# One product in place of two where a half block's edges are spread over the position one-hots

## The reference

```python
xn = _layernorm(x)
h = xn @ W_layer.T + b_layer
a1, a2 = h @ w_a1.T + b_a1, h @ w_a2.T + b_a2
v = leaky_relu(a1[src] + a2[dst], negative_slope=0.01)
ev = exp(v - segment_max(v, src)[src])
gnn = segment_sum((ev / segment_sum(ev, src)[src])[:, None] * h[dst], src)
x = x + gnn + linear_attention(xn)        # 8 heads, features elu + 1
x = x + slice_attention(_layernorm(x))    # 8 heads, 64 slices
```

## Time and profile before

| | us |
|---|---|
| median of 3 runs | 1741.72 (1740.88 to 1742.45) |
| the profiled execution | 1743.75 |
| its span, first to last instruction | 1741.9 |
| PE busy | 1405.2 |
| DVE busy | 1340.7 |
| POOL busy | 1133.4 |
| ACT busy | 662.8 |

### The profile page before, as it was taken

One profiled execution on the slowest core, in us unless ns is written; L12 is line 12 of the kernel. 1 busy time (PEld: TensorE's weight loads), 2 busy tenths in 40 slices (PEclk: granted clock), 3 DMA queues, 4 the chain that ended last, 5 costly groups with the idle time before them and its releaser, 6 DMA issues. The chain is left out here.

```text
span 1741.9 us, 27653 instructions
## 1 busy us (share of the span) xinstructions
PE 1405.2 (81%) x8473; PEld 1112.0 (64%) x8473; DVE 1340.7 (77%) x4033; ACT 662.8 (38%) x1867; POOL 1133.4 (65%) x1196
## 2 busy tenths in 40 slices
PE   5449888885598888898888888888888888887699
PEld 3237777764477666676666666666666666765487
DVE  8898999994488777788777777778777877884244
ACT  0014434340355444454444444444444444441000
POOL 0038888886777777777777777777777777740000
PEclk8659999996599999999999999999999998998599
DMA  9801111112344444444444444444444444520722
GB/s 93 147 5 57 51 46 57 45 52 55 105 121 120 119 121 120 120 119 120 120 123 117 120 121 116 117 121 118 115 120 121 120 117 119 146 69 23 293 74 74
DMA packets 118355, 180.11 MB, mean 103 GB/s; under 512 B 41727, under 2 KB 90238, under 8 KB 118207
## 3 DMA queue, kind: packets, MB, share of 16 engines
q0 software_dynamic: 44384, 113.26, 25.0%
q1 hardware_dynamic: 62735, 45.22, 12.3%
q10 hardware_dynamic: 11088, 19.87, 3.1%
HBM read 142.98 MB, written 35.29 MB: 102 GB/s over the span
## 5 line engine op out<-in xcount | busy, mean ns | idle before, releaser
L1043 POOL DMA_INDIRECT big<-node_table,rest x850 | 857.6, 1009 | 245.6 <-issue 231.5
L1114 PE MATMUL psum<-big 128*125 128x257 f32 x1700 | 428.2, 409 | 79.4 <-DVE big L1613 79.4
L1114 PEld LDWEIGHTS psum<-big 128*125 128x125 f32 x1700 | 337.8, 204 | 142.0 <-DVE big L1613 86.3
L1262 ACT ACTIVATE rest<-big,rest 128x125 f32<-128x125 bf16 x850 | 267.5, 489 | 146.3 <-DVE rest L1561 146.3
L337 POOL DMA_INDIRECT edge_groups<-rest x112 | 141.8, 1266 | 79.6 <-DVE rest L760 52.1
L1613 DVE TENSOR_SCALAR big<-big,rest 128x125 f32<-128x125 bf16 x850 | 171.7, 290 | 0.0
L1568 DVE TENSOR_REDUCE rest<-rest 128x125 f32<-128x2125 f32 x50 | 118.3, 2367 | 32.5 <-ACT rest L1262 32.5
L1142 PE MATMUL psum<-rest,big 125*128 125x126 f32 x416 | 74.1, 333 | 72.0 <-DVE big L1532 72.0
L1142 PEld LDWEIGHTS psum<-rest,big 125*128 125x128 f32 x416 | 63.5, 233 | 90.8 <-DVE big L1532 89.6
L1253 ACT COPY big<-psum 125x1024 bf16<-125x1024 bf16 x150 | 103.7, 762 | 38.1 <-PE psum L1091 38.1
L1149 PE MATMUL psum<-big 125*128 125x256 f32 x416 | 101.0, 386 | 0.0
(11 more groups left out here) (390 smaller groups left out, 2714.4 us busy)
## 6 DMA issues: line engine op xcount, KB each, us to landing
big<-node_table,rest POOLq DMA_INDIRECT x850
slice_weights<-rest ACTq DMA_DIRECT2D x52, 252.0 KB
big<-slice_weights ACTq DMA_DIRECT2D x25, 252.0 KB, 6.9
big<-slice_weights SPq DMA_DIRECT2D x25, 252.0 KB, 7.2
node_table<-big SPq DMA_DIRECT2D x50, 126.0 KB
normalised_turned<-big SPq DMA_DIRECT2D x50, 125.0 KB
rest<-normalised_turned SPq DMA_DIRECT2D x50, 125.0 KB, 2.4
out_dram<-rest SPq DMA_DIRECT2D x50, 125.0 KB
```

Source lines behind the costliest of these rows:

```text
L1043: pool.indirect_dma_start(Gt[:, u, q * TW:(q + 1) * TW], None, table, bass.IndirectOffsetOnAxis(ap=item[:, u, 2 * q:2 * q + 1], axis=0)).t ...
L1114: mm = pe.matmul(bank[bAgg][0:R, 0:D + 1], P[:, u, q, :], Gt[:, u, q * TW:q * TW + D + 1], start=q == 0, stop=q == Q - 1)
L1262: act.activation(V[:, :, q], O[:, u, q, 0:R], ACT.Copy, scale=score[:, u, q:q + 1]).then_inc(s_v, 1)
```

## The change

`spread` makes both halves of `moved` by one instruction of 28 x 128 = 3584 elements per partition instead of two of 28 x 64 = 1792. Its first input is `pos_hot`, read twice for each column (once per digit); its second is the pair of digits, each repeated over 64 positions. For this the digits of an edge stand side by side in one tile `codes` (low, low, high, high), of which `low2` and `high2` are now views; L649, L651 and the memsets of the unused columns write through them. `moved_made` counts two per half instead of three.

```diff
-            low2, high2 = b.take(128, JW, 2, dtype=F16), b.take(128, JW, 2, dtype=F16)
+            codes = b.take(128, JW, 4, dtype=F16)
+            low2, high2 = codes[:, :, 0:2], codes[:, :, 2:4]
...
                     def put(n, h):
-                        pe.wait_ge(moved_made, 3 * (2 * n + h + 1))
+                        pe.wait_ge(moved_made, 2 * (2 * n + h + 1))
...
                         if n + 1 < NB:
-                            pe.wait_ge(moved_made, 3 * (2 * n + 1))
+                            pe.wait_ge(moved_made, 2 * (2 * n + 1))
                             block_starts(n + 1)
...
                     def spread(k, h):
-                        dve.wait_ge(moved_made, 3 * (2 * k + h))
+                        dve.wait_ge(moved_made, 2 * (2 * k + h))
...
                         dve.wait_ge(hot_pos, 2 * k + h + 1)
-                        for f, of in enumerate((low2, high2)):
-                            dve.tensor_tensor(twos(moved[:, h, :, 64 * f:64 * (f + 1)]), twos(pos_hot),
-                                              pairs(of[:, at, :], HW, 64), ALU.mult).then_inc(moved_made, 1)
+                        dve.tensor_tensor(moved[:, h].rearrange("p j (f a b) -> p j f a b", f=2, b=2),
+                                          twos(pos_hot).unsqueeze(2).to_broadcast([128, HW, 2, 32, 2]),
+                                          codes[:, at].rearrange("p j (f b) -> p j f b", f=2).unsqueeze(3).to_broadcast(
+                                              [128, HW, 2, 32, 2]), ALU.mult).then_inc(moved_made, 1)
```

## The result

| | before | after |
|---|---|---|
| median, 18 runs each, same chip (us) | 1741.54 (1738.41 to 1745.35) | 1745.89 (1742.45 to 1751.77) |
| profiled execution, span (us) | 1741.9 | 1745.5 |
| mean granted clock of TensorE | 0.910 | 0.911 |
| last scatter of the sort ends (us from the start) | 417.1 | 420.6 |
| start of one block to the next, mean from 157 to 390 us | 23.21 | 23.75 |

The changed kernel is slower: its time is 1.0024 of the one before, 95% interval 1.0015 to 1.0034, or 4.3 us. Forecast were 1732.0, and a range of 1728 to 1742; the result lies above it. The sign was wrong. The difference arises in the sort: its last scatter ends 3.5 us later, the first gather of the item loop starts at 427.2 for 424.2, and the span ends 3.6 later.

A forecast was written before the change was run, and what follows sets the result against it. VectorE was taken to set the sort's period. Its saving of 11.0 us (product and stalls), less 1.3 given back in POOL's last block, left 9.7 us: 1732.0 us from the median of 1741.72, range 1728 to 1742.

The forecast's parts named there:

- The product itself: Spread on DVE: one product of 3584 elements takes 2.02 us, saving 0.14 us a block.
- the operand forms: Merged product's new repeated operands: keep L741's pace, 2.02 us; far bound 4.07 us at one element per step.
- the layout: L649 and L651 writing pairs in steps of four: nothing to 1.78 us each, before an idle 6.53 us, costing nothing.
- Rival 2: Merged product on DVE falls to one element per step, 4.07 us: 53 us on top, 1785 us; chance 0.05.
- The stalls: DVE's spread beside POOL's products: four stalls of 0.53 us a block become two; 1.15 us saved in eight blocks.
- The 11 us on the spread of VectorE: VectorE's saving up to the last block: 8 x 1.15 + 3 x 0.55 + 0.14 = 11.0 us.
- POOL is then 1.1 us late: POOL at the next block's first L349: 18.75 us, where it could go at 17.65; the lateness doesn't grow.
- the 21.7 that I forecast: Sign in a middle block of the sort: a period near 21.7 us.
- Rival 3: POOL becomes the bound, let in later at two vanished boundaries: 0.63 us more a block, 1749 us; chance 0.08.
- its deciding point: POOL's lateness passing 1.9 us, within which L349 is still inside the first L741; the replay stays at 1.06.
- PE must follow: PE's second put: 0.98 us of idle room, late by at most 0.16 us, so 1.06 to 1.22 us saved a block.
- The tail: Last block of the sort: POOL's scatters end it and come late, giving back 1.3 us; range 0 to 2.5.

The follow-up runs named there:

- order of three: Changed kernel with POOL's scatters issued three instead of two behind each unit: 1730.33 us, 0.9928 of the kernel before; a second run 1728.63 us, 0.9911.
- third buffer: Changed kernel with three instead of two buffers for the scatters' edges and slots: 2351.39 us on the slower chip, 1.0015 of the kernel before, sort 411.1.
- quiet merged kernel: Changed kernel with POOL's two tensor products per unit cut to one column of 256: 2327.94 us, 0.9922 of the kernel before, sort 398.4.
- filled kernel: Changed kernel with 24 small products on PE ahead of its wait for the first half: 2366.86 us, 1.0048 of the kernel before, sort 420.8.

## Why the prediction was wrong, point by point

- *The product itself, the operand forms, the layout*: right. 2.02 us undisturbed, 2.55 with a stall; the layout alone changed nothing. Rival 2 is out.
- *The stalls*: right for the spread. Four a block became two, 24.2 us became 12.4, the last product is never stalled, POOL's waits fall as replayed. The 11 us on the spread of VectorE were there (11.8 by the stalls).
- *The step that failed* is the sentence that POOL is then 1.1 us late and that this "doesn't grow, because POOL's operations from that boundary on, none of them shut out, end 11.8 us later". I replayed only DVE's long instructions and asked whether POOL's lateness comes back to them. POOL came where the replay had it: the unit's products were to start 18.75 us after the block's start and start at 18.79 (197.62). But DVE is at another place by then: it is 1.2 us earlier (L756 at 17.99, before L754 at 19.18). This opens two costs that the sum didn't have. The first is the short instructions of the unpack and of split_places, stretched by 0.5 to 0.8 us each, 2.34 in a long block, 8.9 in the sort for 2.7 before. The unpack had POOL's products beside it before, too, and what differs is a fraction of a microsecond: in the block of the earlier trace rows L756 (223.83) started 0.16 us before the end of L349 (223.27 to 223.99), and L757, the next, 0.10 ahead of L353 (224.07); now L759 starts 0.07 us behind the start of a product and is held until its end. The second is the wait of L771 for the last scatter's landing, 8.4 us in the sort for 1.7 before. The rows for that wait, 221.74, 224.22 and the landing after 2.1 us, were in the trace of before, 0.38 us of room; the prediction didn't use them and nowhere named `scattered`, by which DVE waits for POOL.
- *How much the two are.* From the changed kernel to its order of three (the first run) the sort is 16.6 us shorter: 7.7 are the wait of L771 (8.4 to 0.7), 7.1 the stalls on short instructions (8.9 to 1.8), and the rest, under 2, is the ranks and the end of the sort. The wait was also taken away alone, by the third buffer; the stretched short instructions never were, and their part is by this account of the rows. The steady period there, 21.53, lies just below the 21.7 that I forecast; that is another kernel than the one forecast, and bears out the replay of the spread, not the forecast.
- *Rival 3* had the sign and was near in size (1749, with a chance of 0.08), the size by luck. Its mechanism was POOL late by the vanished boundaries, which is right, and its deciding point, 1.9 us of lateness at the next L349, was wrong: the thing reached first was the landing of the scatter, at 0.38 us. The rule of the lock (the Trainium skill, SBUF — State Buffer, "SBUF: two separate sides") fits the rows of both kernels in the spread. By that rule a longer holder shuts POOL out for longer, and the trace agrees (scatters of 2.58 and 2.73 us where the earlier trace rows have 1.65 and 1.80); what came of it was set by who waits for POOL.
- *PE must follow*: the second put's wait is gone, as forecast. The first put's grew to 4.2 us in the wake of the long blocks, and half-clock stretches follow it, which the prediction didn't consider.
- *The tail*: the sort ended 27.55 us after its last block's start before, and 26.44 after, so 1.1 us were gained here where the sum had 1.3 given back.
- *Chances*: 0.13 for slower was too small for a saving in which POOL's waiting times are longer and only one of its customers was followed.

The short instructions beside the products at 331 us in the order of three aren't stretched for the same reason as in the kernel before: there L758 starts 0.15 us before the end of L350 (330.97 to 331.70), L759 ends as L354 (331.77) begins, and the instructions beside the rest of L354 read PSUM.

Open are: what stretches L758 at 197.07, why the scatter's landing takes 2.8 us there, why PE's ranks come 1.2 us late in the quiet merged kernel, and why the total with the third buffer doesn't follow its sort. Untested is the smallest remedy that the code offers. Only L779 writes the slots that the scatters read; the wait stands three instructions ahead of it, at L771, which writes a buffer that no scatter reads. Moved to L779 it would come 1.84 us later (201.34 for 199.50), more than six of the seven waits of the sort.

## What to carry to other kernels

When an engine gets faster or holds a shared resource for longer at a time, list everybody who waits for the other engine, its DMA landings and the reuse of its buffers too, each with its room in us; the smallest room decides, here 0.38 us, against 1.7 us by which POOL fell behind VectorE at that point. A replay of one block must run over all its instructions and into the second block after it, where a double buffer comes round. And where a hand-written order interleaves two kinds of work, try the order before the instruction: here it was worth 9 to 11 us in the sort with no change of the work at all. And look whether a wait stands directly ahead of the instruction that needs it (not tried here).

## What the runs showed of the hardware

- POOL's scatters take 0.96 us alone and 2.58 to 2.73 us when they are issued inside a long DVE instruction of the spread; they wait for the end of the instruction and push nothing back (the L740 of 184.89, beside a scatter that ends at 185.70, takes its 1.09 us).
- A short DVE instruction of 0.2 us with all its operands in SBUF that starts beside a running product of POOL is held until the product's end: in the 16 traces with whole products, 113 of them start up to 0.5 us behind a product's start (110 to 415 us), and all but one end 0.02 to 0.14 us behind its end. Of 311 that start up to 0.25 us ahead of one, six are stretched (L722 at 201.43 is one). L756, L762, L771, L774 and L710, which read PSUM, keep their durations in all 18 traces.
- One half-clock stretch of TensorE, 3.4 us at 0.50 behind a wait of 2.9 us, costs a block of the filled kernel about 1.0 us.
- A DVE instruction that waits for the landing of a POOL scatter starts 0.08 us behind it; the landing comes 2.1 us after the issue at the least.
- POOL and DVE can fall into a pattern over two blocks, 25.0 and 22.7 us, whose mean is worse than either order's steady block (22.86 before, 21.53 in the order of three).
